# One program for two attention layers, and expert rows gathered inside the attention that follows

## Chip, cores and metric

The kernel runs on one core of a Trainium2 chip. The metric is the device time of one execution in microseconds (us).

## What is computed

Activations x of 8 batches x 256 tokens x 256 features (float32) pass four layers; each adds an attention over a context and then a feed-forward block, both on the layer-normalised x:

```python
x = x + _L0_xattn_ref(_layernorm(x, axis=-1), ctx_1024, ctx_1024, ...)
x = x + _L0_ffn_ref(_layernorm(x, axis=-1), ...)      # 16 gated experts, 2 per token
x = x + _L1_xattn_ref(_layernorm(x, axis=-1), ctx_1024, ctx_1024, ...)
x = x + _L1_ffn_ref(_layernorm(x, axis=-1), ...)      # 8 experts, the last of 2 chosen
x = x + _L2_xattn_ref(_layernorm(x, axis=-1), ctx_1024, ...)
x = x + _L2_ffn_ref(_layernorm(x, axis=-1), ...)      # attention of x to itself, routed
x = x + _L3_xattn_ref(...); x = x + _L3_ffn_ref(...)
```

The "feed-forward" block of layer 2 is itself an attention of 16 heads of 16:

```python
q_norm = q / jnp.linalg.norm(q, axis=-1, keepdims=True)
q_scaled = (q_norm + query_embedding[None]) * jax.nn.softplus(temperature)[None]
attn = jax.nn.softmax(jnp.einsum('bhqd,bhkd->bhqk', q_scaled, k) / math.sqrt(hd), axis=-1)
h = jnp.einsum('bhqk,bhkd->bhqd', attn, v)      # then merged to rows of 256
gates = jax.nn.softmax(h @ Wr.T + br, axis=-1)  # 3 of 15 are kept
sw = jax.nn.softmax(h @ Ws.T + bs, axis=-1)
out = (h * masked_gates.sum(axis=-1, keepdims=True)) @ Wp.T + bp
```

## The kernel before

The program is a sequence of stages, each a block in which PE, DVE, ACT, POOL and SP have their own instruction streams and meet by semaphores; no engine starts a stage before all have left the last. The order is load, **a0** (attention, `attention16`), **f0** (`sorted_gated_experts`), **a1** (retention, `retention16`), **f1** (`sorted_experts`), **a2** (`attention16` with biases), **f2** (`attention16` with keys and values from x, and with the router), **a3** (`attention64`), **f3** (`truncated_experts`), store. x stays in SBUF (`g.x`, "g_x_all") through all of them, 16 tiles of 128 tokens by 256; so do the statistics of each tile (`g.stats`).

**attention16** (L290) is a software pipeline over the 8 batches. `head_steps` (L274) writes out steps s = -1 to 12, each of 8 slots. A slot holds the scores of two heads of batch s-3 (L655), the maxima of two heads of batch s-2 (L634, reduced by DVE at L806), and the extras that a table lists by slot, with the number of batches they lag: normalise ("norm", POOL, L206), transpose ("xT", L230), projections q, k, v (L580, L587), out and the product with wo ("y", added to x at L215 or L836). Each engine walks through the same list in this order and does its own part, so an operation that waits holds back all behind it on its engine. SP moves q and the negated maxima through HBM ("q_out", "q_in", "neg0_out" and so on) to reach other partitions. With 8 batches, the first five steps fill the pipeline and the last five drain it. In the routed form each batch has besides: squares of q, their sums, and the roots by one POOL `pow` (L498) on 128x32, and the gate (logits, three largest, exponentials, factor), mostly on DVE. The stage begins with `norm_factors` (L170), which makes mean and inverse deviation of all 16 tiles at once on DVE, with one root on ACT, and with two memsets on POOL, of KP and v (L473, L474). The routed one computes softplus of the temperature first (L512 to L706).

**retention16** (L1208) has the same form; its q and k are added up from parts by DVE (L1518), and POOL splits them (L1329) and applies causal masks (L1336).

**The experts** (f0 at L1840, f1 at L2290) sort the tokens by expert: POOL scatters the rows of x to slots in HBM, the experts run over tiles of 128 slots, and their rows go to `y_slots`. At the end POOL gathers for every token its rows back with indirect DMAs of 128x256: two for each tile in f0 (L1994, 32 in all), one in f1 (L2426, 16). The loops that issue them are the last work of the stage; DVE weighs and adds the rows to x as halves or tiles land, and takes the statistics for the next norm.

## Time and profile before

| what | value |
|---|---|
| median of 3 runs (range) | 2100.21 us (2098.96 to 2108.5) |
| profiled execution: device time | 2091.46 us |
| profiled execution: span | 2089.7 us |
| PE busy (share of the span) | 1607.8 us (77%) |
| PE weight loads busy | 1235.2 us (59%) |
| DVE busy | 996.2 us (48%) |
| ACT busy | 674.8 us (32%) |
| POOL busy | 512.9 us (25%) |
| mean granted TensorE clock | 0.858 |

The span is the time between the first and last instruction in the trace; it lies 1.8 us under the execution's own time. Busy shares are means over all stages. By the first instruction of each stage the stages begin, in us from the span's start, at 16.0 (a0), 233.0 (f0), 475.9 (a1), 698.3 (f1), 969.3 (a2), 1205.3 (f2), 1507.9 (a3), 2032.4 (f3).

### The profile page before, as it was taken

How to read it: one execution, taken by the hardware profiler on the slowest of the kernel's cores; microseconds unless marked ns; L12 is line 12 of the kernel's file. 1: busy time of each engine (PE TensorE's matmuls, PEld its weight loads, DVE VectorE, ACT ScalarE, POOL GpSimd, SP SyncE). 2: the span in 40 equal slices, each digit the busy share in tenths (PEclk: the TensorE clock that was granted, in tenths of full speed). 3: DMA queues.
4: the chain of work that ended last, by engine and by line, in shares of the span. 5: the costliest groups of instructions: out<-in, count | busy, mean ns of one | idle time of the engine just before them, and what ended most of it. 6: DMA issues, size and time to landing. Idle time of an engine off the chain costs nothing. (4 is left out here: it accounts for less than half of the span.)

```text
span 2089.7 us, 33375 instructions
## 1 busy us (share of the span) xinstructions
PE 1607.8 (77%) x12250; PEld 1235.2 (59%) x12250; DVE 996.2 (48%) x2190; ACT 674.8 (32%) x1408; POOL 512.9 (25%) x583
## 2 busy tenths in 40 slices
PE   4898775905888519981699746888699999999976
PEld 2565654804566418871466434655478888888766
DVE  2675262524454422113366446776426554455542
ACT  1464342302555101111366413434332222222111
POOL 2110043052444020005331064431042223222110
PEclk8798797957999659995799967988799999999986
DMA  4230553435644258852756034442110000000001
GB/s 135 68 83 18 185 213 105 135 91 153 141 112 92 75 204 295 301 197 86 166 130 133 3 85 108 103 92 53 44 55 7 6 7 1 6 6 2 1 7 41
DMA packets 89430, 195.54 MB, mean 94 GB/s; under 512 B 13536, under 2 KB 62176, under 8 KB 80704
## 3 DMA queue, kind: packets, MB, share of 16 engines
q1 hardware_dynamic: 76352, 173.07, 28.9%
q0 software_dynamic: 4608, 12.59, 1.8%
q10 hardware_dynamic: 8320, 7.87, 1.1%
q8 instruction: 96, 1.57, 0.3%
q14 instruction: 54, 0.44, 0.1%
HBM read 136.47 MB, written 57.02 MB: 93 GB/s over the span
## 5 line engine op out<-in xcount | busy, mean ns | idle before, releaser
L806 DVE TENSOR_REDUCE a_sb_mx<-a_mx 128x2 f32<-128x512 f32 x256 | 164.8, 686 | 97.7 <-PE a_mx L634 97.4
L1161 DVE RECIPROCAL a_sb_rden<-a_ot 128x256 f32<-128x256 f32 x64 | 112.1, 1752 | 146.6 <-PE a_ot L1047 146.5
L558 ACT ACTIVATE a_sb_probs<-a_ex 128x512 f32<-128x512 f32 x256 | 139.2, 598 | 103.9 <-PE a_ex L655 103.3
L230 PE MATMUL a_gp<-g_ident,a_sb_xn 128*128 128x128 f32 x128 | 25.1, 329 | 163.0 <-POOL a_sb_xn L206 80.0
L230 PEld LDWEIGHTS a_gp<-g_ident,a_sb_xn 128*128 128x128 f32 x128 | 16.9, 165 | 167.5 <-DMA a_sb_bo<-a_bo 70.9
L806 DVE TENSOR_REDUCE f_sb_mx<-f_mx 128x2 f32<-128x512 f32 x128 | 82.2, 684 | 36.7 <-PE f_mx L634 36.3
L558 ACT ACTIVATE f_sb_probs<-f_ex 128x512 f32<-128x512 f32 x128 | 69.5, 597 | 71.5 <-PE f_ex L655 71.4
L990 ACT ACTIVATE a_sb_probs<-a_sc 128x512 f32<-128x512 f32 x64 | 38.2, 597 | 167.9 <-PE a_sc L1035 111.7
L959 POOL TENSOR_SCALAR_AFFINE_SELECT a_sb_probs<-a_sb_probs 128x256 f32<-128x256 f32 x128 | 49.2, 409 | 164.9 <-ACT a_sb_probs L991 164.8
L655 PE MATMUL a_ex<-a_sb_QP,a_sb_KP 49*128 49x256 f32 x512 | 68.1, 343 | 24.8 <-ACT a_sb_probs L558 21.3
L952 POOL TENSOR_TENSOR a_sb_q_lo<-a_sb_whole,a_sb_q_hi 128x512 fp32r<-128x512 f32 x32 | 40.7, 1271 | 180.0 <-ACT a_sb_q_hi L981 180.0
L2488 PE MATMUL f_hb<-f_sb_xsT,f_sb_wb 128*128 128x128 f32 x640 | 76.0, 281 | 10.9 <-ACT f_sb_xsT L2441 10.9
L2488 PEld LDWEIGHTS f_hb<-f_sb_xsT,f_sb_wb 128*128 128x128 f32 x640 | 74.3, 196 | 13.1 <-issue 6.6
L980 ACT ACTIVATE a_sb_whole<-a_gp 128x512 f32<-128x512 f32 x64 | 38.3, 598 | 134.5 <-PE a_gp L999 134.5
L655 PEld LDWEIGHTS a_ex<-a_sb_QP,a_sb_KP 49*128 49x128 f32 x512 | 42.2, 197 | 63.9 <-issue 40.2
L634 PE MATMUL a_mx<-a_sb_KP,a_sb_QP 48*128 48x256 f32 x512 | 62.7, 322 | 17.4 <-DVE a_sb_mx L806 16.3
L668 PE MATMUL a_ot<-a_sb_probs,a_sb_v 128*32 128x256 f32 x1024 | 74.1, 410 | 0.0
L2602 DVE TENSOR_SCALAR f_sb_hT<-f_hb,f_sb_wb 128x128 f32<-128x128 f32 x80 | 22.5, 344 | 105.3 <-PE f_hb L2488 105.3
L1336 POOL TENSOR_SCALAR_AFFINE_SELECT a_sb_sim<-a_sb_sim 128x256 f32<-128x256 f32 x128 | 49.9, 418 | 89.0 <-ACT a_sb_sim L1390 89.0
L2497 PE MATMUL f_yb<-f_sb_wb,f_sb_hT 128*128 128x256 f32 x320 | 70.7, 379 | 0.0
L1146 DVE TENSOR_REDUCE a_sb_mx<-a_sc 128x2 f32<-128x256 f32 (+1 forms) x128 | 62.1, 544 | 11.6 <-PE a_sc L1020 11.6
L2497 PEld LDWEIGHTS f_yb<-f_sb_wb,f_sb_hT 128*128 128x128 f32 x320 | 60.0, 190 | 7.7
(427 smaller groups left out, 3929.5 us busy)
## 6 DMA issues: line engine op xcount, KB each, us to landing
f_sb_wb<-f_w SPq DMA_DIRECT2D x20, 2052.0 KB, 11.3
a_sb_kvT<-ctxT SPq DMA_DIRECT2D x32, 256.0 KB, 3.5
a_q_moved<-a_sb_qs SPq DMA_DIRECT2D x16, 512.0 KB, 3.5
a_sb_QP<-a_q_moved SPq DMA_DIRECT2D x32, 256.0 KB, 4.7
f_x_slots<-f_sb_zero SPq DMA_DIRECT2D x1, 6144.0 KB, 20.1
f_sb_xs<-f_x_slots SPq DMA_DIRECT2D x20, 256.0 KB, 2.8
f_y_slots<-f_sb_ys ACTq DMA_DIRECT2D x20, 256.0 KB, 2.6
a_sb_QP<-a_q_moved SPq DMA_DIRECT2D x32, 128.0 KB, 5.0
```

The costliest lines, as they stand in the source:

```text
L230: op = pe.transpose(out[:, k, t * P:(t + 1) * P], xn[:, t, k * P:(k + 1) * P], g.ident[:])
L558: act.activation(probs[:, group % 3, 2 * (u % 2) + par], EX[par][:], ACT.Exp, scale=scale)\
L634: op = pe.matmul(MX[par][:, t, :], QP[at:at + R, b % 3, u, t * P:(t + 1) * P], KP[at:at + R, b % KB, u % KM, :], start=True, stop=True)
L655: op = pe.matmul(EX[par][:, t, :], KP[at:at + R + 1, b % KB, u % KM, t * P:(t + 1) * P], QP[at:at + R + 1, b % 3, u, :], start=True, stop= ...
L668: op = pe.matmul(OT[c // 2][32 * j:32 * j + 32, c % 2, :], v4[:, b % 4, t, (4 * c + j) % VH, :], probs[:, (4 * b + c) % 3, j, t, :], start ...
L806: dve.tensor_reduce(mx[:, :, column(2 * u + par)], MX[par][:], AX.X, ALU.max, negate=True)\
L959: op = pool.affine_select(later, later, [[0, 2], [1, P]], ALU.is_ge, 0.0, base=0, channel_multiplier=-1)
L1146: op = dve.tensor_reduce(mx[:, t, 2 * i:2 * i + 2], SC[pair][:, :, t, 0:(t + 1) * P], AX.X, ALU.max, negate=True)
L1161: dve.reciprocal(rden[:, n], OT[n][:, 1, :])
L1336: op = pool.affine_select(later, later, [[0, 2], [1, P]], ALU.is_ge, 0.0, base=0, channel_multiplier=-1)
L2488: op = pe.matmul(HB[j % 2][c // (FC // 2)][:, c % (FC // 2), :], w1(j, k, c), xsT[:, j, k, :], start=(k == 0), stop=(k == KD - 1))
L2497: op = pe.matmul(YB[j % 2][:, 0], hT[:, j, c, :], w2(j, c), start=(c == 0), stop=(c == FC - 1))
```

## The change

1. a2 and f2 become one call of `attention16` over 16 batches: batch 8+i is batch i of the routed layer, whose x is what batch i of a2 has left. The steps are 22 where they were 14 and 14. Both layers' weights lie in SBUF.
2. The gathers of f0 and f1 leave the experts' stages. `Arrival` issues them batch by batch on POOL within the first steps of a1 and of the merged stage, by the table `ARRIVALS` (step: batches gathered, batches added). DVE adds them and takes the statistics. Norm factors are then computed for one or two batches at a time by `batch_norm_factors`, with a Newton iteration instead of ACT's root: on DVE in a1, on POOL in the merged stage, there also for each routed batch.
3. The maxima of a pair of heads are one PSUM tensor and one DVE reduction of 128x1024 where two of 128x512 stood.
4. In routed batches the roots of q's sums are a Newton iteration on POOL (14 operations of 128x32) instead of one `pow`; squares and the copies of the negated maxima go from DVE to ACT; the query embedding is added as a bias of ACT's split of q; the gate's exponentials are six small ACT operations that also sum. "norm", "v" and "scale" change slots.
5. KP is filled by DVE; of v POOL fills columns 16 to 31 only.

Order of the instructions: POOL, from the tail of f0 into a1 (`sb_xn`, `sb_xnT` receive the first and second expert's rows). Before:

```order
L1994 DMA f_sb_xn<-f_y_slots,f_sb_pos 128x256
L1994 DMA f_sb_xnT<-f_y_slots,f_sb_pos 128x256
L1856 UNCONDITIONAL_BRANCH
L1321 UNCONDITIONAL_BRANCH
L1323 MEMSET a_sb_v 128x3072
L1329 TENSOR_TENSOR a_sb_q_parts<-a_sb_q_whole,a_sb_q_parts 128x512
L1329 TENSOR_TENSOR a_sb_k_parts<-a_sb_k_whole,a_sb_k_parts 128x512
L1344 TENSOR_TENSOR g_x_all<-g_x_all,a_sb_bo 128x512
L1329 TENSOR_TENSOR a_sb_q_parts<-a_sb_q_whole,a_sb_q_parts 128x512
```

With the change:

```order
L2146 UNCONDITIONAL_BRANCH
L1473 UNCONDITIONAL_BRANCH
L249 DMA a_sb_landing<-f_y_slots,g_pos 128x256 x16
L1482 TENSOR_TENSOR a_sb_q_parts<-a_sb_q_whole,a_sb_q_parts 128x512
L1482 TENSOR_TENSOR a_sb_k_parts<-a_sb_k_whole,a_sb_k_parts 128x512
L1497 TENSOR_TENSOR g_x_all<-g_x_all,a_sb_bo 128x512
L249 DMA a_sb_landing<-f_y_slots,g_pos 128x256 x8
L1482 TENSOR_TENSOR a_sb_q_parts<-a_sb_q_whole,a_sb_q_parts 128x512
L1482 TENSOR_TENSOR a_sb_k_parts<-a_sb_k_whole,a_sb_k_parts 128x512
L1497 TENSOR_TENSOR g_x_all<-g_x_all,a_sb_bo 128x512
L249 DMA a_sb_landing<-f_y_slots,g_pos 128x256 x8
```

The tail has no gather left; sixteen stand ahead of POOL's first split of q in a1, eight ahead of the second.

PE, where a2 gives over to f2 (`a_ex` scores, `a_mx` maxima, `a_gp` all small products). Before:

```order
L655 MATMUL a_ex<-a_sb_QP,a_sb_KP 128x256 x4
L587 MATMUL a_gp<-a_sb_wo,a_sb_oT 128x256 x4
L668 MATMUL a_ot<-a_sb_probs,a_sb_v 32x256 x8
L678 MATMUL a_gp<-g_ident,a_sb_oraw 128x128 x8
L230 MATMUL a_gp<-g_ident,a_sb_otm 128x128 x4
L587 MATMUL a_gp<-a_sb_wo,a_sb_oT 128x256 x4
L308 UNCONDITIONAL_BRANCH
L575 UNCONDITIONAL_BRANCH
L230 MATMUL f_gp<-g_ident,f_sb_xn 128x128 x4
L587 MATMUL f_gp<-f_sb_wq,f_sb_xnT 128x256 x4
```

With the change, the end of step 8, in which the first routed batch (8) enters, and the start of step 9:

```order
L305 MATMUL a_gp<-g_ident,a_sb_qtm 128x128 x4
L742 MATMUL a_gp<-a_sb_wo,a_sb_oT 128x256 x4
L806 MATMUL a_ex<-a_sb_QP,a_sb_KP 128x256 x4
L785 MATMUL a_mx<-a_sb_KP,a_sb_QP 128x256 x4
L305 MATMUL a_gp<-g_ident,a_sb_xn 128x128 x4
L794 MATMUL a_gp<-g_ident,a_sb_mx 8x128 x2
L819 MATMUL a_ot<-a_sb_probs,a_sb_v 32x256 x8
L806 MATMUL a_ex<-a_sb_QP,a_sb_KP 128x256 x4
L785 MATMUL a_mx<-a_sb_KP,a_sb_QP 128x256 x4
L742 MATMUL a_gp<-a_sb_wq,a_sb_xnT 128x256 x4
```

Batch 8's q is transposed beside batch 4's product with wo, and batch 9's transposes and q stand among the scores of batch 6 and the maxima of batch 7. Before, a2 had run empty before f2's first transpose.

POOL, one full step of routed batches. Before:

```order
L483 TENSOR_TENSOR f_sb_qs<-f_sb_qf,f_sb_qs 128x512
L498 TENSOR_TENSOR f_sb_qn<-f_sb_qn,f_sb_half 128x32
L483 TENSOR_TENSOR f_sb_ks<-f_sb_kf,f_sb_ks 128x512
L504 TENSOR_TENSOR g_x_all<-g_x_all,f_sb_bo 128x512
L206 TENSOR_SCALAR f_sb_xn<-g_x_all,g_ln_mean,g_ln_rstd 128x256 x2
```

With the change, from the norm on (L1338 to L1344 follow twice more, then L632, the bias L639 and the split of q):

```order
L209 TENSOR_SCALAR a_sb_xn<-g_x_all,g_ln_mean,g_ln_rstd 128x256 x2
L597 TENSOR_TENSOR a_sb_ks<-a_sb_kf,a_sb_ks 128x512
L1320 TENSOR_SCALAR a_sb_qn<-a_sb_qn 128x32
L1338 TENSOR_TENSOR a_sb_qn<-a_sb_qn 128x32
L1340 TENSOR_TENSOR a_sb_qn<-a_sb_qn 128x32
L1342 TENSOR_SCALAR a_sb_qn<-a_sb_qn 128x32
L1344 TENSOR_TENSOR a_sb_qn<-a_sb_qn 128x32
```

The `pow` (L498) gives way to 14 operations, and 21 more (L220 to L1344, on 128x2) stand ahead of each norm.

The diff, cut to its core:

```diff
+def batch_norm_factors(eng, g, first, last, ln):
+    at = slice(first * TT, (last + 1) * TT)
+    ln = ln[:, :, 0:at.stop - at.start]
+    st = lambda i: g.stats[:, at, i]
+    eng.tensor_tensor(ln[:, 0, :], st(1), st(4), ALU.add)
+    eng.tensor_tensor(ln[:, 1, :], st(1), st(4), ALU.subtract)
+    eng.tensor_tensor(ln[:, 2, :], st(2), st(5), ALU.add)
+    eng.drain()
+    eng.tensor_scalar(g.mean[:, at], ln[:, 0, :], 0.5, None, ALU.mult)
+    eng.tensor_tensor(ln[:, 1, :], ln[:, 1, :], ln[:, 1, :], ALU.mult)
+    eng.tensor_scalar(ln[:, 2, :], ln[:, 2, :], 1.0 / D, EPS, ALU.mult, ALU.add)
+    eng.drain()
+    eng.tensor_scalar(ln[:, 1, :], ln[:, 1, :], 0.25, None, ALU.mult)
+    eng.drain()
+    eng.tensor_tensor(ln[:, 3, :], ln[:, 1, :], ln[:, 2, :], ALU.add)
+    eng.drain()
+    root_guess(eng, g.rstd[:, at], ln[:, 3, :])
+    for _ in range(3):
+        root(eng, g.rstd[:, at], ln[:, 3, :], g.rstd[:, at], ln[:, 4, :])
...
+class Arrival:
+    def __init__(self, sb, sem, landed, layer):
+        self.layer, self.n = layer, 2 - layer
+        self.rows = sb("landing", [P, 2, self.n, TT, D])
+        self.landed, self.taken, self.arrived = landed, sem("taken"), sem("arrived")
+    def gather(self, pool, g, b):
+        at_least(pool, self.taken, b - 1)
+        for t in range(TT):
+            for i in range(self.n):
+                pool.indirect_dma_start(self.rows[:, b % 2, i, t, :], None, g.y_slots[self.layer],
+                                        bass.IndirectOffsetOnAxis(g.pos[self.layer][:, i, b * TT + t:b * TT + t + 1], 0))\
+                    .then_inc(self.landed[b % 2], 16)
+    def add(self, dve, g, b):
+        dve.wait_ge(self.landed[b % 2], 16 * TT * self.n * (b // 2 + 1))
+        xb = g.x[:, b * TT:(b + 1) * TT, :]
+        if self.layer == 1:
+            dve.tensor_tensor(xb, xb, self.rows[:, b % 2, 0], ALU.add).then_inc(self.taken, 1)
+            dve.drain()
+        else:
+            for i in range(2):
+                for t in range(TT):
+                    op = dve.scalar_tensor_tensor(out=xb[:, t], in0=self.rows[:, b % 2, i, t, :],
+                                                  scalar=g.weight[:, i, b * TT + t:b * TT + t + 1], in1=xb[:, t],
+                                                  op0=ALU.mult, op1=ALU.add)
+                if i == 1:
+                    op.then_inc(self.taken, 1)
+                dve.drain()
+        next_stats(dve, g, b).then_inc(self.arrived, 1)
+        dve.drain()
+ARRIVALS = {-1: ([0, 1], [0]), 0: ([2, 3], [1]), 1: ([4, 5], [2, 3]), 2: ([6, 7], [4, 5]), 3: ([], [6, 7])}
+def arrivals(s):
+    gathers, adds = ARRIVALS.get(s, ([], []))
+    return [("gather", b) for b in gathers] + [("arrive", b) for b in adds] + [("factors", b) for b in adds[-1:]]
...
-ROUTED_EXTRAS = {0: [("neg1", 3), ("xT", 0), ("weigh3", 4), ("y", 5)], 1: [("q", 0), ("square", 0), ("out1", 4)],
-                 2: [("weigh0", 3), ("T0", 4), ("T1", 4)], 3: [("k", 0)], 4: [("neg0", 2), ("weigh1", 3), ("aT", 4)],
-                 5: [("scale", 0), ("gate", 4), ("v", 0), ("out0", 3), ("norm", -1)], 6: [("weigh2", 3), ("gexp", 4)],
-                 7: [("qT", 0), ("factor", 4)]}
+ROUTED_EXTRAS = {0: [("neg1", 3), ("xT", 0), ("weigh3", 4), ("y", 5)], 1: [("q", 0), ("out1", 4), ("norm", -1)],
+                 2: [("square", 0), ("weigh0", 3), ("T0", 4), ("T1", 4)], 3: [("k", 0), ("sums", 0)],
+                 4: [("neg0", 2), ("weigh1", 3), ("aT", 4), ("roots", 0)], 5: [("gate", 4), ("out0", 3)],
+                 6: [("weigh2", 3), ("gexp", 4), ("v", 0), ("scale", 0)], 7: [("qT", 0), ("factor", 4)]}
...
+                    if what == "gather":
+                        rows_in_flight.gather(pool, g, b)
+                        if b == 1:
+                            fill_ones()
+                    elif what == "factors":
+                        pool.wait_ge(rows_in_flight.arrived, b + 1)
+                        batch_norm_factors(pool, g, first_of(b), b, ln)
+                    elif what == "norm":
+                        if b >= B:
+                            pool.wait_ge(stats_ready, b - B + 1)
+                            batch_norm_factors(pool, g, b % B, b % B, ln)
                         if b >= 1:
                             full(pool, "xT", b - 1)
-                        normalise(pool, g, b, xn, xn_ready)
-                    elif what == ("qT" if router else "q"):
+                        normalise(pool, g, b % B, xn, xn_ready)
...
-                    elif what == "square":
-                        pool.wait_ge(q_sums, b + 1)
-                        pool.tensor_tensor(qn[:, 2], qn[:, 0], half[:], ALU.pow).then_inc(q_roots, 1)
+                    elif what == "roots":
+                        r = b - of(b).first
+                        pool.wait_ge(q_summed, r + 1)
+                        if r == 0:
+                            pool.wait_ge(centre, 1)
+                        else:
+                            pool.wait_ge(q_scaled, r)
+                        root_guess(pool, qn[:, 3], qn[:, 0])
+                        for _ in range(3):
+                            root(pool, qn[:, 3], qn[:, 0], qn[:, 3], qn[:, 1])
+                        by_token = lambda a: a.rearrange("p (t h) -> p t h", t=TT)
+                        pool.tensor_tensor(by_token(qn[:, 2]), by_token(qn[:, 3]),
+                                           spq[:, 0:H].rearrange("p (a h) -> p a h", a=1).broadcast_to([P, TT, H]),
+                                           ALU.mult).then_inc(q_rooted, 1)
...
+                    elif what == "square":
+                        act.wait_ge(q_biased, b - of(b).first + 1)
+                        act.activation(qsq[:], qtm[:], ACT.Square).then_inc(q_squared, 1)
                     elif what == "qT":
-                        split_rows("qT", b, qf, qs, q_split, q_out, None)
+                        if b == of(b).first:
+                            act.wait_ge(centre, 1)
+                        split_rows("qT", b, qf, qs, q_split, q_out, qe)
+                    elif what.startswith("neg") and routed(b):
+                        half_ = number(what)
+                        full(act, what, b)
+                        if b >= 1:
+                            act.wait_ge(neg_out[half_], 16 * b)
+                        act.activation(negT[:, half_, :], GP[bank][0:8, 0, :], ACT.Copy).then_inc(gp_read[bank], 1)
...
-                        act.wait_ge(gate_in, b + 1)
-                        act.activation(le[:, :, 0:H + 1], lg[:, :, 0:H + 1], ACT.Exp).then_inc(gate_exp, 1)
+                        act.wait_ge(gate_in, b - of(b).first + 1)
+                        for t in range(TT):
+                            act.activation(le[:, t, 0:H - 1], lg[:, t, 0:H - 1], ACT.Exp, bias=neg_top[:, t, 0:1],
+                                           accum_out=sums[:, t, 0:1])
+                            act.activation(le[:, t, H + 1:H + 4], top[:, t, 0:3], ACT.Exp, bias=neg_top[:, t, 0:1],
+                                           accum_out=sums[:, t, 1:2])
+                            op = act.activation(le[:, t, H - 1:H + 1], lg[:, t, H - 1:H + 1], ACT.Exp,
+                                                bias=neg_top[:, t, 1:2], accum_out=sums[:, t, 2:3])
+                        op.then_inc(gate_exp, 1)
...
+                        at_least(pe, mx_read, 8 * b + u)
                         for t in range(TT):
                             for par in range(2):
                                 at = 64 * par
-                                op = pe.matmul(MX[par][:, t, :], QP[at:at + R, b % 3, u, t * P:(t + 1) * P],
+                                op = pe.matmul(MX[:, par, t, :], QP[at:at + R, b % 3, u, t * P:(t + 1) * P],
                                                KP[at:at + R, b % KB, u % KM, :], start=True, stop=True)
-                                if t == TT - 1:
-                                    op.then_inc(mx_full[par], 1)
+                                if t == TT - 1 and par == 0:
+                                    op.then_inc(mx_full, 1)
+                        op.then_inc(mx_full, 1)
...
-                            dve.wait_ge(mx_full[par], 8 * b + u + 1)
-                            dve.tensor_reduce(mx[:, :, column(2 * u + par)], MX[par][:], AX.X, ALU.max, negate=True)\
-                               .then_inc(mx_read[par], 1)
-                    elif what.startswith("neg"):
+                        dve.wait_ge(mx_full, 2 * (8 * b + u + 1))
+                        pair = mx[:].rearrange("p t (i g h) -> p g t i h", i=2, g=2)[:, :, :, u // 4, u % 4]
+                        dve.tensor_reduce(pair, MX[:], AX.X, ALU.max, negate=True).then_inc(mx_read, 1)
...
-            centre_values()
             for step in steps:
                 for what, b in step:
                     bank = gp.slot((what, b)) if what in small else None
-                    if what in ("qr", "kr"):
+                    if what == "arrive":
+                        rows_in_flight.add(dve, g, b)
+                    elif what == "factors":
+                        batch_norm_factors(dve, g, first_of(b), b, ln)
...
-            for half_ in range(2):
-                for t in range(half_ * NT // 2, (half_ + 1) * NT // 2):
-                    for i in range(2):
-                        pool.indirect_dma_start(rows[i][:, t, :], None, y_slots,
-                                                bass.IndirectOffsetOnAxis(pos[:, i, t:t + 1], 0))\
-                            .then_inc(gathered[half_], 16)
...
-            pool.wait_ge(scattered, 16 * NT)
-            for t in range(NT):
-                pool.indirect_dma_start(rows[:, t, :], None, y_slots, bass.IndirectOffsetOnAxis(pos[:, t:t + 1], 0))\
-                    .then_inc(gathered[2 * t // NT], 16)
...
-                attention16(nc, g, s, w, bias=True)
+                layers = [(sub(io, n + "_"), n == "f2") for n in ("a2", "f2") if n in stages]
+                attention16(nc, g, s, layers, arriving="f1" in stages)
-            elif s == "f2":
-                attention16(nc, g, s, w, bias=True, kv_from_x=True, router=True)
```

## Rows read from the trace of the kernel before

**Rows 1.** Busy time by stretch: us, PE, PEld, DVE, ACT, POOL busy (x), PEclk, DMA share, GB/s.
```profile
424.00:475.85 51.85, 0.00 (x0) 0.00 (x0) 18.44 (x48) 0.00 (x0) 30.42 (x32) 0.50 0.29 81
969.26:1205.30 236.04, 184.44 (x1440) 123.86 (x1440) 121.93 (x220) 113.18 (x228) 58.23 (x43) 0.88 0.45 106
1205.30:1508.50 303.20, 222.00 (x1536) 148.87 (x1536) 189.19 (x468) 114.47 (x225) 103.26 (x52) 0.79 0.32 76
1073.00:1136.80 63.80, 61.26 (x542) 41.51 (x544) 42.42 (x79) 41.04 (x84) 16.17 (x13) 1.00 0.57 131
1340.10:1400.90 60.80, 52.62 (x386) 34.81 (x384) 44.23 (x112) 26.77 (x54) 23.32 (x12) 0.84 0.41 94
```

**Rows 2.** Timeline, tail of f0: start, duration, engine, [idle before it <- what ended it].
```profile
423.54 0.98 POOL L1994 DMA_INDIRECT f_sb_xn<-f_y_slots,f_sb_pos  x1 [87.32 <-issue]
...
462.92 0.94 POOL L1994 DMA_INDIRECT f_sb_xnT<-f_y_slots,f_sb_pos  x1 [0.30 <-issue]
...
475.86 2.66 POOL L1323 MEMSET a_sb_v<- 128x3072 f32 x1 [11.99 <-POOLq L140]
```

**Rows 3.** Timeline, tail of f1 and the first work of a2.
```profile
940.80 0.97 POOL L2426 DMA_INDIRECT f_sb_rows<-f_y_slots,f_sb_pos  x1 [177.41 <-issue]
...
949.62 0.95 POOL L2426 DMA_INDIRECT f_sb_rows<-f_y_slots,f_sb_pos  x1 [0.30 <-issue]
...
952.34 2.29 DVE L2614 TENSOR_TENSOR g_x_all<-g_x_all,f_sb_rows 128x2048 f32<-128x2048 f32 x1 [15.07 <-DMA f_sb_rows<-f_y_slots,f_sb_pos]
953.37 2.08 POOL L2426 DMA_INDIRECT f_sb_rows<-f_y_slots,f_sb_pos  x1 [0.30 <-issue]
...
969.26 5.22 POOL L473 MEMSET a_sb_KP<- 128x6144 f32 x1 [7.55 <-POOLq L140]
969.76 4.75 DVE L177 TENSOR_SCALAR g_ln_mean<-g_ln_mean 128x16 f32<-128x16 f32 x1
```

**Rows 4.** Timeline, fill of a1: first transpose, then the q of batch 0 and batch 3.
```profile
488.28 1.12 PE L230 MATMUL a_gp<-g_ident,a_sb_xn 128*128 128x128 f32 x4 [70.51 <-DMA a_sb_bo<-a_bo]
...
497.58 0.69 DVE L1518 TENSOR_TENSOR a_sb_q_whole<-a_sb_part 128x512 f32<-128x512 f32 x1
...
543.89 0.69 DVE L1518 TENSOR_TENSOR a_sb_q_whole<-a_sb_part 128x512 f32<-128x512 f32 x1
```

**Rows 5.** Busy time of a1's first 68 us (columns of rows 1).
```profile
475.85:543.90 68.05, 48.10 (x300) 36.11 (x304) 26.94 (x49) 27.74 (x57) 24.00 (x34) 0.84 0.70 173
```

**Rows 6.** Timeline, fill of a2: transposes of batches 0 and 2.
```profile
981.24 1.12 PE L230 MATMUL a_gp<-g_ident,a_sb_xn 128*128 128x128 f32 x4 [44.43 <-POOL a_sb_xn L206]
...
1011.05 1.09 PE L230 MATMUL a_gp<-g_ident,a_sb_xn 128*128 128x128 f32 x4 [4.08 <-POOL a_sb_xn L206]
```

**Rows 7.** Timeline, what is added to x in a2: batches 0 and 7.
```profile
1073.02 0.69 DVE L215 TENSOR_TENSOR g_x_all<-g_x_all,a_gp 128x512 f32<-128x512 f32 x1 [0.74 <-PE a_gp L587]
...
1202.86 0.69 DVE L215 TENSOR_TENSOR g_x_all<-g_x_all,a_gp 128x512 f32<-128x512 f32 x1 [4.56 <-PE a_gp L587]
```

**Rows 8.** Timeline, the same in f2: batches 0 and 3, and the start of a3.
```profile
1340.09 0.87 DVE L836 SCALAR_TENSOR_TENSOR g_x_all<-f_gp,f_sb_sm,g_x_all 128x256 f32<-128x256 f32 x2 [2.17 <-PE f_gp L587]
...
1429.76 0.88 DVE L836 SCALAR_TENSOR_TENSOR g_x_all<-f_gp,f_sb_sm,g_x_all 128x256 f32<-128x256 f32 x2 [2.50 <-PE f_gp L587]
...
1507.93 0.18 DVE L173 TENSOR_TENSOR g_ln_mean<-g_ln_stats 128x16 f32<-128x16 f32 x1 [0.76 <-PEq L140]
```

**Rows 9.** Timeline of f2: end of its softplus chain; the roots of one batch.
```profile
1215.41 0.43 DVE L706 TENSOR_TENSOR f_sb_qe<-f_sb_qe,f_sb_spq 128x256 f32<-128x256 f32 x1
...
1345.63 5.45 POOL L498 TENSOR_TENSOR f_sb_qn<-f_sb_qn,f_sb_half 128x32 f32<-128x32 f32 x1 [10.28 <-DVE f_sb_qn L719]
```

**Rows 10.** Lines of POOL: busy us, mean ns of one | idle before.
```profile
L504 POOL TENSOR_TENSOR g_x_all<-g_x_all,f_sb_bo 128x512 f32<-128x512 f32 x8 | 10.2, 1279 | 0.0
L476 POOL MEMSET f_sb_half<- 128x32 f32 x1 | 0.1, 143 | 0.0
```

**Rows 11.** The page's costliest groups: the maxima of a0 and a2.
```profile
L806 DVE TENSOR_REDUCE a_sb_mx<-a_mx 128x2 f32<-128x512 f32 x256 | 164.8, 686 | 97.7 <-PE a_mx L634 97.4
```

412 lines of the change are left out of this document (216 added, 196 removed).

## Prediction

> **What bounds the kernel now.** The table of stages came first: no engine is busy throughout, and PE's 77% is a mean over stages of which some are bound by PE and some are not. So the stages that the change touches were read one by one, each by busy time in a window and then by the timeline at its ends.
>
> The tails of f0 and f1 are bound by one queue. In f0's last 51.85 us PE and ACT do nothing, POOL is busy for 30.42 us with 32 gathers, and DVE for 18.44 us with the adds and statistics [rows 1]. The first gather starts at 423.54 and the last, at a pitch of 1.25 us, at 462.92; a1 begins at 475.86 [rows 2]. In f1 16 gathers start at 940.80, and a2 begins at 969.26 [rows 3].
>
> a2 in its full steps is bound by PE: 61.26 us busy of 63.80 in three steps, with the clock at 1.00, so 21.27 us a step. f2 in its full steps is not: PE is busy 52.62 of 60.80 us at a clock of 0.84 and DVE 44.23, so a step takes 30.4 us while no engine fills it [rows 1]. The step holds a chain from engine to engine, of which one link is the `pow` on POOL, 5.45 us [rows 9]. Both stages also fill and drain: a2 takes 103.8 us from its start to its first y and f2 134.8 us [rows 1, 3, 7, 8].
>
> **The sum, part by part,** against the profiled execution (span 2089.7 us, device time 2091.46 us).
>
> *Gathers out of f0, into a1.* a1 starts when the experts' last rows are written, at about 424.3 in place of 475.86: 51.5 us less [rows 2]. Some comes back. Ahead of the first transpose, 12.4 us after a1's start now [rows 2, 4], stand four gathers at 1.25 us (5.0), the landing (1.8, from the eighth gather's end at 950.57 to the add at 952.34 [rows 3]), the adds and statistics of one batch (18.44 / 8 = 2.3 [rows 1]), 17 drained rounds of small operations at about 0.25 us (an estimate; the smallest single operation shown takes 0.18 [rows 8]), 4.3, and the norm: some 14.7, so +2.3. Behind it DVE does in steps 0 to 3 what it did in the tail, 2.3 us a batch, and four more sets of factors at 4.7 to 5.1: 7.0 + 3 x 9.7 = 36 us. a1's first 68 us have 41 us in which DVE is idle (26.94 busy of 68.05 [rows 5]), but PE is busy 48.10 of it and waits for DVE's q in order: the q of batch 0 to 3 are 46.3 us apart in sum [rows 4]. An add that waits for its landing holds the k and q sums queued behind it on DVE, and PE waits for those. I take 60% exposed, 22 us; the bounds are 10 (nearly all in the idle time) and 40 (all of it, and a wait). POOL's sixteen gathers end 20 us after the start, and its first split of q was due at 21.7 [rows 4], so POOL adds nothing there. **Net -27.5 us** (-39 to -9).
>
> *Gathers out of f1, into the merged stage.* The stage starts at 941.5 in place of 969.26. Its y of batch 0 came 103.8 us later; now the first transpose comes not 12.0 us after the start [rows 3, 6] but about 22.5: softplus stands ahead of the adds on DVE (its end is 10.6 us into f2 [rows 1, 9]; 12 with more loads), then add and statistics 1.6, 21 small POOL operations at 0.3 (below), 6.3, and the norm 2.5. The fill steps, 14.9 us from transpose to transpose [rows 6], get a POOL load of 4 gathers (5.0), factors (6.3), norm (2.5) and three operations of 1.28 [rows 10], 17.6 us: two steps give +5.4, and 1 for the third. So y of batch 0 comes at 941.5 + 103.8 + 17 = 1062.3, with 8 and 30 as bounds of the 17.
>
> A gather beside DVE's add of two SBUF operands took 2.08 us instead of 0.95 [rows 3]; eight of these would be 9 us more on POOL, within the upper bound. The Trainium skill ("SBUF — State Buffer", Who interferes with whom) has the two share one port pair that locks the loser out, but infers that this form of DVE operation leaves a gather's descriptors alone: those 9 us would then be nought. The trace speaks against that inference.
>
> *Fill and drain merged.* Three steps more with a2's work alone are 63.8 us [rows 1]: the end of step 7 is at 1126.1. Steps 8 to 15 carry in the same slots a routed batch coming in and an older one being scored. PE's work of a step in f2 is 26.3 us at clock 0.84, so 22.1 at full clock; DVE's is 22.1 (44.23 / 2) and loses squares, copies and gate operations; a2's step is 21.3 [rows 1]. The latency that made 30.4 us of it was the chain within one step; roots now have a slot of their own, v and scale come two slots later. I take 24 us, PE's 22.1 and gaps like a2's (2.5 in three steps) twice over: 192 us. The bounds are 21.3 and 30.4, 170 and 243. The drain from there is f2's: 78.2 us from its y of batch 3 to the start of a3 [rows 8], against 68.5 for the same stretch in a2 (1136.8 to 1205.3 [rows 1]); with the lighter gate I take 71. Together 1126.1 + 192 + 71 = 1389.1, in place of 1507.9. **-118.8 us** (-160 to -60).
>
> *Maxima.* Two reductions of 686 ns [rows 11] become one of about 1.3 us that starts when both halves are there. 192 pairs change, 64 of them in a0. DVE saves perhaps 0.07 us a pair and starts 0.1 later: 0, with -13 and +7 as bounds. *Memsets.* DVE's KP fill runs under the loads and beside softplus; POOL's goes. 0; without that cover it costs its 5.22 us once [rows 3]. *POOL's price.* No row shows an operation of two inputs on 128x32 or smaller. The ends are 0.14 us (a memset, no input) and 1.28 us (128x512, 16 times the columns) [rows 10]; I take 0.3, near the lower since the columns are few, with room for the drain. Roots and factors are 35 such, 10.5 us a step, on top of f2's 23.32 / 2 - 5.45 = 6.2 [rows 1, 9]: 16.7 us, under the 24.
>
> [...]
>
> Sum: -27.5 - 118.8 = -146.3, so 2091.5 - 146.3 = 1945.2 for the profiled execution. That one lay 8.7 under the median of the runs (2100.21), so **1954 us**.
>
> As a check: the merged stage would take 448 us, and a2 and f2 hold 184.4 + 222.0 = 406 us of busy PE, part of it at clocks of 0.88 and 0.79 [rows 1]. PE would be busy nine tenths of the time, which a2 alone reaches only in full steps; a higher clock shortens the 406, so it can be met, but not bettered by much.
>
> **The rivals.** *Cheaper than taken (0.13):* the routed step runs at a2's pace and a1 hides the adds: 8 x 2.5 + 10 = 30 less, 1924. For it speaks that PE's own work is 22.1; against it that f2's three full steps average 29.9 [rows 8]. *a1's fill gives it all back (0.08):* DVE waits for landings in order, and so do q and k; the 27.5 shrink to 0: 1982. For it, the 36 us on an engine on which PE's q depends; against it, DVE's 41 idle. *POOL becomes the pace of the merged stage (0.12):* it decides once 6.2 + 35p is over 24, from p = 0.51 us for a small drained operation. At p = 0.6 the step is 27.2 and the factors and roots of the fill and drain, 84 operations or so, cost 25 more: +51, 2005. For it speaks that the nearest two-input row is 1.28 and `pow` on the same tile takes 5.45; against it the memset's 0.14. *Slower (0.05):* the same operation at p = 0.86 or more: 8 x (35p - 17.8) + 84 x (p - 0.3) passes 146; at p = 1.0 it is 197, 2151. The place is POOL in steps 8 to 15, with PE waiting for transposes of xn. Only the distance of 1.28 from 0.3 allows it. *The forecast:* 0.62.
>
> **The numbers.** Range 1912 to 2012: the forecast with its bounds, the cheap case, a1's case and the milder half of POOL's. About 0.5% (10 us) is what a measurement of this kernel can tell from no change; only the slower case and the worst part of POOL's reach it. Faster 0.94, same 0.01, slower 0.05.
>
> **What would show it.** Small POOL operations under 0.35 us each; a routed full step of 23 to 25 us with PE's idle time below 3; the first transpose of a1 some 15 us and of the merged stage some 22 us after their starts; y of batch 0 about 121 us after the start. Wrong would be: PE in the merged stage waiting on POOL's xn at every step, a1 longer than 222.4 + 40 us, or a routed step near 30 with all engines partly idle, which would say that the chain and not the missing overlap set f2's pace.

## The result, and the profile after

The changed kernel takes 1969.81 us (median of 4 runs, 1968.33 to 1970.33) against 2102.89 us before (4 runs, 2098.96 to 2108.5). The ratio is 0.9364, its 95% interval 0.9339 to 0.9389: faster by 6.4%. Here and below, an execution over 1.5% longer than the fastest of its kernel is left out of the comparison; this concerns one of the run with two maxima and one of the kernel before. The forecast was 1954 us; the measured time lies 16 us above it, within the range.

The profiled execution took 1968.33 us, 123.1 less than the one of before. Its page, busy time of each engine:

```profile
span 1966.5 us, 33821 instructions
PE 1566.8 (80%) x12250; PEld 1211.7 (62%) x12250; DVE 956.5 (49%) x1948; ACT 688.7 (35%) x1527; POOL 533.5 (27%) x954
```

PE does the same 12250 products in 41 us less of busy time, at a mean clock of 0.88 in place of 0.858. The stages, from the first instruction of each, in us:

| stage | before | after | difference | forecast |
|---|---|---|---|---|
| a0 | 217.1 | 209.6 | -7.4 | 0 |
| f0 | 242.9 | 192.0 | -50.9 | -51.5 |
| a1 | 222.4 | 253.0 | +30.6 | +24 |
| f1 | 271.0 | 244.7 | -26.3 | -27.8 |
| a2 and f2, merged | 538.6 | 469.6 | -69.0 | -91 |
| a3, f3, store | 581.8 | 581.8 | 0.0 | 0 |

Busy time by stretch (columns as in [rows 1]) of a1's first 68 us, and of the merged stage: start to y of batch 0, three steps of a2's work alone, the eight steps with routed batches, the drain.

```profile
417.40:485.45 68.05, 28.72 (x116) 21.63 (x116) 45.62 (x147) 12.43 (x24) 39.18 (x40) 0.70 0.70 186
915.00:1048.50 133.50, 71.07 (x444) 50.35 (x446) 52.50 (x66) 40.86 (x86) 73.17 (x149) 0.73 0.56 138
1048.50:1111.46 62.96, 60.53 (x542) 41.23 (x544) 40.95 (x54) 40.98 (x84) 26.18 (x55) 1.00 0.58 132
1111.46:1304.50 193.04, 175.23 (x1532) 119.74 (x1534) 136.92 (x209) 123.20 (x294) 98.34 (x279) 0.99 0.48 109
1304.50:1384.68 80.18, 59.16 (x464) 37.35 (x462) 37.42 (x99) 38.18 (x109) 0.00 (x0) 0.83 0.13 28
```

The eight steps took 193.0 us where 192 were forecast: 24.1 each, PE busy 21.9 of them at a granted clock of 0.99. In f2 PE had been busy 26.3 of 30.4 us at 0.84 [rows 1], so the idle gaps are down from 4.1 to 2.2 us a step, and with the clock up the products themselves take 4.4 us less. The two ends are dearer than forecast: 133.5 us to the first y against 121, and 80.2 for the drain against 71. In a1 DVE is busy 45.6 of 68 us where it was 26.9 [rows 5], and PE only 28.7 where it was 48.1.

Timeline of the merged stage, POOL alone, from three of the fill steps (start, duration, then in brackets the idle time before and what ended it):

```profile
941.96 0.19 POOL L222 TENSOR_TENSOR a_sb_ln<-g_ln_stats 128x2 f32<-128x2 f32 x1
943.74 0.23 POOL L224 TENSOR_SCALAR g_ln_mean<-a_sb_ln 128x2 f32<-128x2 f32 x1 [1.59 <-issue]
...
960.42 0.94 POOL L249 DMA_INDIRECT a_sb_landing<-f_y_slots,g_pos  x1 [0.30 <-issue]
...
961.69 0.20 POOL L222 TENSOR_TENSOR a_sb_ln<-g_ln_stats 128x4 f32<-128x4 f32 x1
...
968.08 0.24 POOL L224 TENSOR_SCALAR g_ln_mean<-a_sb_ln 128x4 f32<-128x4 f32 x1 [6.18 <-issue]
...
984.94 0.96 POOL L249 DMA_INDIRECT a_sb_landing<-f_y_slots,g_pos  x1 [0.30 <-issue]
...
986.24 0.20 POOL L222 TENSOR_TENSOR a_sb_ln<-g_ln_stats 128x4 f32<-128x4 f32 x1
...
993.56 0.24 POOL L224 TENSOR_SCALAR g_ln_mean<-a_sb_ln 128x4 f32<-128x4 f32 x1 [7.13 <-issue]
```

Between L222 and L224 the code has one `drain`. Three times it follows on four gathers, and three times POOL stands still, 1.6, 6.2 and 7.1 us. How long the gathers of the second group were on their way, by the view of line L249 in that window:

```profile
DMA to landing us min/median/max: 7.3/8.7/9.5
```

The last of them started at 960.42 and took 7.3 us to land, so it was there at 967.7; the operation behind the drain started at 968.08. At the other two places the last gather started at 940.69 and 984.94 and took 2.7 and 8.3 us: there at 943.4 and 993.2, with the next operation at 943.74 and 993.56. Each time POOL goes on 0.3 us behind the last landing, so the drain seems to last until the gathers have landed. No engine is named as the releaser ("issue"), so this was a theory until an experiment had moved the gathers.

What PE sees of it are the transposes of batches 0, 1 and 2:

```profile
936.68 1.12 PE L305 MATMUL a_gp<-g_ident,a_sb_xn 128*128 128x128 f32 x4 [28.00 <-POOL a_sb_xn L209]
...
956.53 1.09 PE L305 MATMUL a_gp<-g_ident,a_sb_xn 128*128 128x128 f32 x4 [9.87 <-POOL a_sb_xn L209]
...
981.02 1.09 PE L305 MATMUL a_gp<-g_ident,a_sb_xn 128*128 128x128 f32 x4 [13.59 <-POOL a_sb_xn L209]
```

The first comes 21.6 us after the stage's start at 915.08, near the forecast 22.5. The next two follow at 19.9 and 24.5 us, not at 14.9 as in a2 before [rows 6], and each time PE has waited for POOL's norm.

In a1 the first add of batch 0, and the first transpose:

```profile
421.92 0.95 POOL L249 DMA_INDIRECT a_sb_landing<-f_y_slots,g_pos  x1 [0.30 <-issue]
...
428.53 1.84 DVE L262 SCALAR_TENSOR_TENSOR g_x_all<-a_sb_landing,g_weight,g_x_all 128x256 f32<-128x256 f32 x4 [9.39 <-DMA a_sb_landing<-f_y_slots,g_pos]
...
437.11 1.09 PE L305 MATMUL a_gp<-g_ident,a_sb_xn 128*128 128x128 f32 x4 [28.19 <-DVE a_sb_xn L209]
```

The fourth gather ended at 422.87 and its rows were there at 428.5, 5.7 us later and not 1.8. The DMA engines are busier here: 0.89 of the time from 418 to 430 us, with a1's weights among the loads, against 0.32 from 940.8 to 952.3 us in the old tail of f1. That this is the cause is likely, but no run shows it alone. The first transpose comes 19.7 us after a1's start, where it was 12.4 [rows 2, 4] and 14.7 had been forecast. The sums of q of batches 0 to 3 come 30.4, 49.0, 75.2 and 96.7 us after the start, before 21.7, 35.8, 50.4 and 68.0. The lag is 8.7 at the first, 24.8 at the third, 28.7 at the fourth, and 29 to 31 for the last four. It arises in the fill and stays.

Prices on POOL, from the view of line L1340 between 1232 and 1304 us (ns, shortest/median/longest, then the first and last start and the shape):

```profile
L1340 POOL TENSOR_TENSOR a_sb_qn<-a_sb_qn x9: 250/252/272, 1244.6 to 1296.2; 128x32 f32<-128x32 f32 x9
L1340 POOL TENSOR_TENSOR a_sb_ln<-a_sb_ln x6: 194/194/196, 1233.2 to 1260.4; 128x2 f32<-128x2 f32 x6
```

The maxima, from the page's costliest groups, 1223 ns a pair where two of 686 stood [rows 11]:

```profile
L951 DVE TENSOR_REDUCE a_sb_mx<-a_mx 128x4 f32<-128x1024 f32 x192 | 234.7, 1223 | 121.2 <-PE a_mx L785 118.7
```

### The profile page after: what moved, and what is told of

Same layout as the page of the kernel before. It is cut to its first block and busy times, and to the rows that moved or that the text cites. A ratio compares the mean times of both kernels' runs of the same rounds, so it can differ in the third digit from the quotient of the medians.

```text
span 1966.5 us, 33821 instructions
## 1 busy us (share of the span) xinstructions
PE 1566.8 (80%) x12250; PEld 1211.7 (62%) x12250; DVE 956.5 (49%) x1948; ACT 688.7 (35%) x1527; POOL 533.5 (27%) x954
## 5 line engine op out<-in xcount | busy, mean ns | idle before, releaser
L951 DVE TENSOR_REDUCE a_sb_mx<-a_mx 128x4 f32<-128x1024 f32 x192 | 234.7, 1223 | 121.2 <-PE a_mx L785 118.7
L706 ACT ACTIVATE a_sb_probs<-a_ex 128x512 f32<-128x512 f32 x384 | 208.8, 598 | 157.3 <-PE a_ex L806 156.7
L806 PE MATMUL a_ex<-a_sb_QP,a_sb_KP 49*128 49x256 f32 x768 | 98.9, 334 | 39.6 <-ACT a_sb_probs L706 29.0
L249 POOL DMA_INDIRECT a_sb_landing<-f_y_slots,g_pos x48 | 46.5, 970 | 288.6 <-POOLq L143 264.8
L305 PE MATMUL a_gp<-g_ident,a_sb_xn 128*128 128x128 f32 x160 | 29.6, 314 | 117.9 <-POOL a_sb_xn L209 76.6
L806 PEld LDWEIGHTS a_ex<-a_sb_QP,a_sb_KP 49*128 49x128 f32 x768 | 60.7, 190 | 94.6 <-issue 57.2
L819 PE MATMUL a_ot<-a_sb_probs,a_sb_v 128*32 128x256 f32 x1536 | 109.3, 404 | 2.1 <-ACT a_sb_probs L706 2.1
L785 PE MATMUL a_mx<-a_sb_KP,a_sb_QP 48*128 48x256 f32 x768 | 88.2, 306 | 13.1 <-DVE a_sb_mx L951 12.4
L785 PEld LDWEIGHTS a_mx<-a_sb_KP,a_sb_QP 48*128 48x128 f32 x768 | 62.3, 195 | 24.4 <-DVE a_sb_mx L951 17.1
L2739 DVE TENSOR_SCALAR f_sb_hT<-f_hb,f_sb_wb 128x128 f32<-128x128 f32 x80 | 22.5, 344 | 105.0 <-PE f_hb L2625 105.0
L597 POOL TENSOR_TENSOR a_sb_qs<-a_sb_qf,a_sb_qs 128x512 fp32r<-128x512 f32 x24 | 31.0, 1291 | 154.1 <-ACT a_sb_qs L661 97.1
```

The lines of the kernel that those rows point to most:

```text
L305: op = pe.transpose(out[:, k, t * P:(t + 1) * P], xn[:, t, k * P:(k + 1) * P], g.ident[:])
L706: act.activation(probs[:, group % 3, 2 * (u % 2) + par], EX[par][:], ACT.Exp, scale=scale)\
L785: op = pe.matmul(MX[:, par, t, :], QP[at:at + R, b % 3, u, t * P:(t + 1) * P], KP[at:at + R, b % KB, u % KM, :], start=True, stop=True)
L806: op = pe.matmul(EX[par][:, t, :], KP[at:at + R + 1, b % KB, u % KM, t * P:(t + 1) * P], QP[at:at + R + 1, b % 3, u, :], start=True, stop= ...
L819: op = pe.matmul(OT[c // 2][32 * j:32 * j + 32, c % 2, :], v4[:, b % 4, t, (4 * c + j) % VH, :], probs[:, (4 * b + c) % 3, j, t, :], start ...
L951: dve.tensor_reduce(pair, MX[:], AX.X, ALU.max, negate=True).then_inc(mx_read, 1)
```

## The experiments

All medians stand beside the change's 1969.81 us. Each run was timed against the kernel before on the same chip; that ratio and its interval are given, to be held against the change's 0.9364 (0.9339 to 0.9389). Lengths of stages are those of the one profiled execution.

**The merge undone.** a2 and f2 are two programs again, each in the new form:

```diff
-                layers = [(sub(io, n + "_"), n == "f2") for n in ("a2", "f2") if n in stages]
-                attention16(nc, g, s, layers, arriving="f1" in stages)
+                attention16(nc, g, s, [(w, False)], arriving="f1" in stages)
+            elif s == "f2":
+                attention16(nc, g, s, [(w, True)])
```

> The merge alone undone: a2 and f2 are again two programs of 8 batches, each in the new form, a2 still with its arrivals. Theory 1 (most of the merge's gain is a fill and a drain that overlap; the routed step of 24.1 us is a property of the routed form, not of the overlap): a2 takes about 133 + 63 + 68 = 264 us, f2 about 125 + 3 x 24 + 80 = 277, together 541 in place of 469.6: about +71, 2040 us. Theory 2 (the overlap itself gave the routed step its pace): f2's full steps are again 30 us and it takes 300, together 564: about +95, 2064 us.

Measured: 2038.03 us (ratio 0.9695, 0.9654 to 0.9737), theory 1's number. The two stages take 534.1 us in place of 469.6. In f2 alone, y of batches 0 to 2:

```profile
1296.47 0.87 DVE L980 SCALAR_TENSOR_TENSOR g_x_all<-f_gp,f_sb_factor,g_x_all 128x256 f32<-128x256 f32 x2 [4.03 <-PE f_gp L742]
1320.75 0.88 DVE L980 SCALAR_TENSOR_TENSOR g_x_all<-f_gp,f_sb_factor,g_x_all 128x256 f32<-128x256 f32 x2 [2.50 <-PE f_gp L742]
1345.18 0.87 DVE L980 SCALAR_TENSOR_TENSOR g_x_all<-f_gp,f_sb_factor,g_x_all 128x256 f32<-128x256 f32 x2 [2.50 <-PE f_gp L742]
```

24.3 and 24.4 us a step without any merge. So the merge as such is worth 64.5 us, one fill against one drain, and the step's pace belongs to the routed form: f2 by itself takes 277.2 us (1171.00 to 1448.21) where it took 302.6. In these two steps PE is busy 22.3 us each at a granted clock of 1.00, so the higher clock too comes with the routed form and not with the merge.

**f0's gathers back in a tail,** a block of their own between f0 and a1:

```diff
+                gather_tail(nc, g, "t0", 0)
-                retention16(nc, g, s, w, arriving="f0" in stages)
+                retention16(nc, g, s, w)
```

> The 32 gathers and adds of f0 stand in a tail of their own again, before a1, which starts with factors for all tiles. Theory 1 (a1 is 30.6 us longer because of the arrivals in its fill, and the tail was 51): a1 is back at 222 to 223 us, the sum about +20, 1990 us. Theory 2 (a1 is longer for another reason, its new memset or other edits): a1 stays near 253 and the whole is about +51, 2020 us.

Measured: 2001.52 us (0.9505, 0.9457 to 0.9553), +32. The tail takes 52.5 us. a1 takes 228.2, not the 222 to 223 of theory 1 and far from theory 2's 253. By the stages the arrivals save 52.5 + 228.2 - 253.0 = 27.7 us. Of the rest, a0 and a3 to the store are 3.6 and 3.3 us longer in this profile, and the edit touches neither. Where a1's 6 us over the kernel before come from is open: its q sums run level with before up to the fourth (69.1 us against 68.0), and the granted clock is 0.87 against 0.89.

**f1's gathers back in a tail,** by the same block for layer 1:

```diff
+                gather_tail(nc, g, "t1", 1)
-                attention16(nc, g, s, layers, arriving="f1" in stages)
+                attention16(nc, g, s, layers)
```

> The 16 gathers and adds of f1 stand in a tail of their own again, the rest is merged as before. Theory 1 (the fill of the merged stage gave all of it back: y of batch 0 came 133.5 us after the start in place of 103.8, the tail was 27): y of batch 0 comes about 107 us after the start, the whole is the same within 5 us, 1970 us. Theory 2, the prediction's (a gain of 27.8 - 17 = 11 us): 1981 us.

Measured: 1972.01 us (0.9389, 0.9345 to 0.9433), the same as the change. The tail takes 28.6 us, and y of batch 0 comes 100.3 us after the start of the merged stage where the change needs 133.5. This part of the change brought nothing: the fill took back what the tail gave.

This tail also has the slow gather of [rows 3] once more, beside the same add of 128x2048 with two operands in SBUF:

```profile
926.81 0.95 POOL L2763 DMA_INDIRECT t_rows<-f_y_slots,g_pos  x1 [0.30 <-issue]
927.05 2.29 DVE L2774 TENSOR_TENSOR g_x_all<-g_x_all,t_rows 128x2048 f32<-128x2048 f32 x1 [18.32 <-DMA t_rows<-f_y_slots,g_pos]
928.07 2.10 POOL L2763 DMA_INDIRECT t_rows<-f_y_slots,g_pos  x1 [0.30 <-issue]
```

It took 2.10 us, and 2.08 before. Both times it started while the add ran and ended 0.8 us behind the add's end, and both times the gather ahead of it, which met the add's beginning, kept its 0.95.

**Factors ahead of the gathers** on POOL, steps 0 to 3 of the merged stage:

```diff
-        steps = [arrivals(i - 1) + step for i, step in enumerate(steps)]
+        rank = {"factors": 0, "gather": 1, "arrive": 2}
+        steps = [(arrivals(-1) if i == 0 else sorted(arrivals(i - 1), key=lambda u: rank[u[0]])) + step
+                 for i, step in enumerate(steps)]
```

> One change of order on POOL in the merged stage: in steps 0 to 3 the factors of the batches added stand ahead of the next gathers, not behind them. Theory 1 (the first drain behind gathers lasts until they have landed: idle 1.6, 6.2 and 7.1 us before L224): these three waits go, y of batch 0 comes about 12 us sooner, about 1957 us. Theory 2 (that idle time is covered, or POOL waits there for something else): the same time within 3 us, 1969, with gaps that remain.

Measured: 1957.43 us (0.9306, 0.9268 to 0.9344), theory 1's number. The same two places of the timeline, where no gather is under way now:

```profile
960.61 0.19 POOL L222 TENSOR_TENSOR a_sb_ln<-g_ln_stats 128x4 f32<-128x4 f32 x1
961.31 0.24 POOL L224 TENSOR_SCALAR g_ln_mean<-a_sb_ln 128x4 f32<-128x4 f32 x1 [0.51 <-issue]
...
979.99 0.19 POOL L222 TENSOR_TENSOR a_sb_ln<-g_ln_stats 128x4 f32<-128x4 f32 x1
980.69 0.24 POOL L224 TENSOR_SCALAR g_ln_mean<-a_sb_ln 128x4 f32<-128x4 f32 x1 [0.51 <-issue]
```

0.51 us in place of 6.2 and 7.1, with the same instructions on the same tiles. y of batch 0 comes 122.1 us after the start, 11.4 sooner. The merged stage as a whole is only 7.4 us shorter in this profile (462.2), since the eight steps and the drain took 196.0 and 81.2 us; the profiled execution is the longest of the four (1966.07).

**Two maxima again,** in a0 and the merged stage:

```diff
-                        dve.wait_ge(mx_full, 2 * (8 * b + u + 1))
-                        dve.tensor_reduce(pair, MX[:], AX.X, ALU.max, negate=True).then_inc(mx_read, 1)
+                        for par in range(2):
+                            dve.wait_ge(mx_full[par], 8 * b + u + 1)
+                            dve.tensor_reduce(pair[:, par], MX[par][:], AX.X, ALU.max, negate=True)\
+                               .then_inc(mx_read[par], 1)
```

> Only the maxima undone: two PSUM tensors and two reductions of 128x512 for a pair of heads, in a0 and in the merged stage. Theory 1 (one reduction takes 1.22 us in place of 2 x 0.686, 0.15 saved a pair on an engine that is seldom last): a0 5 to 8 us longer, routed steps up to 1 us longer, together about +10, 1979 us. Theory 2 (the single reduction is what brought the routed step from 30 to 24 us): eight routed steps of 27 or more, +30 or more.

Measured: 1981.03 us, the middle of three from 1964.41 to 1986.02 (0.939, 0.9319 to 0.9462). The interval holds the change's 0.9364, so the times alone show no difference. In its profile a0 takes 217.0 us as before, steps of a2's work alone are 21.26 us, near the old length and not 20.97, and the eight steps with routed batches take 194.8 us against 193.0. So the single reduction gives 0.2 to 0.3 us a step of eight pairs and is not what brought 30 to 24; the 7 us in a0 agree with theory 1, but a0 also varied from 207 to 215 us between profiles of kernels that have it unchanged.

**One pow again** for the roots of the routed batches:

```diff
-                        root_guess(pool, qn[:, 3], qn[:, 0])
-                        for _ in range(3):
-                            root(pool, qn[:, 3], qn[:, 0], qn[:, 3], qn[:, 1])
+                        pool.tensor_tensor(qn[:, 3], qn[:, 0], half[:], ALU.pow)
+                        pool.drain()
```

> Only the roots of the routed batches changed: one power of -0.5 on POOL in place of the guess and three Newton steps (13 operations at a pitch of 0.34 us, 4.4 us). Theory 1 (the slot in the table matters, not the operation, since pow takes 5.45): the same time within 4 us, 1970 us, routed steps of 24 to 25. Theory 2 (the pow itself held f2's steps up): steps of 27 or more, +25 us and more. Theory 3 (small operations on POOL are what costs): faster by 5 us or more.

Measured: 1979.25 us (0.9424, 0.938 to 0.9468), +9.4, between theories 1 and 2; the interval just meets the change's. The merged stage is 9.2 us longer, and four routed steps in the middle are 26.3, 25.5, 25.3 and 23.3 us, in the change 24.3, 24.2, 23.2 and 23.5: about 1.2 us a step for an operation that takes 5.46 us against 13 that take 4.4.

**Squares and negated copies back on DVE** in routed batches:

```diff
-                        act.wait_ge(q_biased, b - of(b).first + 1)
-                        act.activation(qsq[:], qtm[:], ACT.Square).then_inc(q_squared, 1)
+                        dve.tensor_tensor(qsq[:], qtm[:], qtm[:], ALU.mult).then_inc(q_squared, 1)
+                        dve.drain()
```

and the copies likewise, by one branch of DVE for all batches.

> In the routed batches the square of q and the two copies of the negated maxima are DVE's again, not ACT's (0.69 + 2 x 0.40 us and a drain a batch). Theory 1 (f2's old step was long because DVE, 22.1 us busy and its drains, kept PE's maxima waiting; at 17.1 of 24.1 there is room for 1.6 more): up to +1 us a step, 1970 to 1978 us. Theory 2 (every us on DVE is on the path): +13 or more. Theory 3 (DVE does not matter): no change, with ACT's 1.5 us a step less.

Measured: 1975.91 us (0.9405, 0.9369 to 0.9442), +6 with a spread of 1969.85 to 1983.15. Theory 1's range, but theory 3 is not excluded: the two intervals overlap, and the merged stage is 472.8 us against 469.6.

**The old slots** with that work on DVE:

```diff
-ROUTED_EXTRAS = {0: [("neg1", 3), ("xT", 0), ("weigh3", 4), ("y", 5)], 1: [("q", 0), ("out1", 4), ("norm", -1)],
-                 2: [("square", 0), ("weigh0", 3), ("T0", 4), ("T1", 4)], 3: [("k", 0), ("sums", 0)],
-                 4: [("neg0", 2), ("weigh1", 3), ("aT", 4), ("roots", 0)], 5: [("gate", 4), ("out0", 3)],
-                 6: [("weigh2", 3), ("gexp", 4), ("v", 0), ("scale", 0)], 7: [("qT", 0), ("factor", 4)]}
+ROUTED_EXTRAS = {0: [("neg1", 3), ("xT", 0), ("weigh3", 4), ("y", 5)],
+                 1: [("q", 0), ("square", 0), ("sums", 0), ("roots", 0), ("out1", 4)],
+                 2: [("weigh0", 3), ("T0", 4), ("T1", 4)], 3: [("k", 0)], 4: [("neg0", 2), ("weigh1", 3), ("aT", 4)],
+                 5: [("scale", 0), ("gate", 4), ("v", 0), ("out0", 3), ("norm", -1)], 6: [("weigh2", 3), ("gexp", 4)],
+                 7: [("qT", 0), ("factor", 4)]}
```

> The routed batches' table of slots as it was (norm, scale and v in slot 5, square, sums and roots right behind q in slot 1), with squares and negated copies on DVE as in the run with DVE's work back. Theory 1 (the slots brought most of the 30.4 to 24.3, because DVE waits less in the middle of its maxima): routed steps of 27 to 30, 1995 to 2025 us. Theory 2 (the slots do not matter; the lighter gate and the roots do): steps near 25, within 5 us of that run's 1976.

Measured: 1997.72 us (0.9511, 0.9493 to 0.9528), 22 over the run with DVE's work back. y of three batches within the routed steps, and busy time between the first and the last:

```profile
1253.91 0.87 DVE L975 SCALAR_TENSOR_TENSOR g_x_all<-a_gp,a_sb_factor,g_x_all 128x256 f32<-128x256 f32 x2 [7.03 <-PE a_gp L734]
1282.28 0.88 DVE L975 SCALAR_TENSOR_TENSOR g_x_all<-a_gp,a_sb_factor,g_x_all 128x256 f32<-128x256 f32 x2 [5.62 <-PE a_gp L734]
1311.81 0.88 DVE L975 SCALAR_TENSOR_TENSOR g_x_all<-a_gp,a_sb_factor,g_x_all 128x256 f32<-128x256 f32 x2 [7.14 <-PE a_gp L734]
```

```profile
1253.91:1311.81 57.90, 48.68 (x386) 32.39 (x386) 36.30 (x71) 30.41 (x80) 27.74 (x80) 0.91 0.40 92
```

28.4 and 29.5 us a step, with DVE busy only 18.2 of them; the other steps are between 24 and 28, but for the one from the last y of a2 to the first routed one, 35.9 us (26.6 in the change). The eight steps take 222.9 us together, against 196.5 in the run with DVE's work back and 193.0 in the change. With the lighter gate but the old order much of f2's old pace is back, and the clock is down to 0.91 with PE's gaps. Moving the operations in the list is worth 22 us here, while what they cost on their engines (the two runs before) is worth 6 and 9 at most, each near what these times can tell. The run moves norm, squares, sums, roots, v and scale at once, so it doesn't say which move counts.

**One arrival in each step,** with the factors first:

```diff
-ARRIVALS = {-1: ([0, 1], [0]), 0: ([2, 3], [1]), 1: ([4, 5], [2, 3]), 2: ([6, 7], [4, 5]), 3: ([], [6, 7])}
+ARRIVALS = {-1: ([0, 1], [0]), 0: ([2], [1]), 1: ([3], [2]), 2: ([4], [3]), 3: ([5], [4]), 4: ([6], [5]), 5: ([7], [6]),
+            6: ([], [7])}
```

> Factors ahead of the gathers on POOL as in the run with that order (1957 us), and one batch arrives in each step (steps 0 to 6) in place of two in steps 1 to 3, in a1 and in the merged stage. Theory 1 (in a1 the arrivals of two batches, 9.7 us of DVE in one fill step, hold back q and k; one batch costs 6.6 and the rest falls where DVE has room): a1 about 8 us shorter, the merged stage 2 to 5, together about 1946 us. Theory 2 (DVE has no room in a1's full steps either, and three more sets of factors cost 4.3 each): a1 5 to 13 us longer, 1960 to 1970 us.

Measured: 1945.89 us (0.926, 0.9222 to 0.9299), theory 1's number. In a1 the table is all that differs from the change (POOL has no factors there): it takes 239.6 us, 13.4 less, and the merged stage 450.0 (469.6; 462.2 with the order alone). The q of batch 3 comes 82.9 us after a1's start in place of 96.7. Three more sets of factors are paid in full steps, where they cost less than what they take out of the fill.

**Batch 0 added ahead of the softplus,** on top of that:

```diff
+            if arriving:
+                rows_in_flight.add(dve, g, 0)
             if L[-1].router:
                 dve.wait_ge(first_in, first_all)
                 dve.wait_ge(softplus, 1)
```

> As the run with one arrival a step (1945.9 us), and in the merged stage batch 0 is added before DVE waits for the softplus, not behind it. Theory 1 (the rows of batch 0 have landed by about 3.5 us before the softplus ends, and the first transpose hangs on that add): y of batch 0 comes 3 us sooner, 1943 us, a difference that the stage's rows can show and the medians hardly. Theory 2 (the landing is later, or another wait is last): nothing.

Measured: 1937.03 us (0.9215, 0.9191 to 0.924), the fastest version. The first y comes 112.0 us after the stage's start in place of 115.4, the 3 us foreseen; the median fell by 9, of which a1 and the merged stage show 2.4, so the rest is most likely the spread of that other run (1938.19 to 1951.87). That version is faster than the change by 33 us.

**a1's factors on POOL,** on top of one arrival a step:

```diff
                     elif what == "factors":
-                        batch_norm_factors(dve, g, first_of(b), b, ln)
+                        pool.wait_ge(rows_in_flight.arrived, b + 1)
+                        batch_norm_factors(pool, g, first_of(b), b, ln)
+                        pool.sem_inc(factored, 1)
```

DVE's norm waits for `factored`, and the factors stand ahead of each step's gathers in a1 too.

> As the run with one arrival a step, and in a1 the norm factors of each batch are POOL's, ahead of its gathers, not DVE's. Theory 1 (a1's fill is bound by DVE, which gets 4.3 us a batch back): a1 5 to 15 us shorter than 239.6, 1931 to 1941 us. Theory 2 (the chain from the add to the norm counts, and 21 operations at a pitch of 0.34 take 7.1 us where DVE's took 4.5): a1 5 to 20 us longer, 1951 to 1966 us.

Measured: 2013.11 us (0.9606, 0.9572 to 0.9641). Theory 2, and three times as bad as it said: a1 takes 304.8 us in place of 239.6. Two of its waits from the start of a1 to 550 us:

```profile
DVE a_sb_xn L209 <- POOLq L1348: 36.5, 5, 8.2
PE a_ot L1638 <- POOL a_sb_sim L1499: 24.4, 3, 12.4
```

DVE's norm waits for POOL five times, 7.3 us on average, about what a set of 21 operations takes. What the expectation had not priced comes on top: POOL's masks of the scores (L1499) stand in order behind the factors, and PE waits up to 12.4 us for them. In the same window POOL itself waits 23.0 us, in six pieces, for DVE's statistics ahead of its sets, and all behind them in its queue waits too.

**The arriving batches' factors on DVE in the merged stage,** on top of the fastest version:

```diff
-                        batch_norm_factors(pool, g, first_of(b), b, ln)
+                        pool.wait_ge(factors, b + 1)
...
+                        batch_norm_factors(dve, g, b, b, ln)
+                        dve.drain()
+                        dve.sem_inc(factors, 1)
```

> As the run with batch 0 added first (1937 us), and in the merged stage the norm factors of the eight arriving batches are DVE's, right behind each add, as in a1; POOL keeps the routed batches' factors. Theory 1 (in the fill the chain from add to norm counts, as a1 with POOL's factors showed from the other side, and DVE does the set in 4.5 us against POOL's 7.1): y of batch 0 about 5 to 10 us sooner, 1929 us. Theory 2 (DVE's maxima and v of the fill then wait behind it as much as the chain gains): the same within 3 us. Theory 3 (DVE, in order, becomes what PE waits for): +5 us or more.

Measured: 1972.97 us (0.939, 0.936 to 0.9419), 36 slower than without this edit; theory 3. In the profile the merged stage has 474.1 us in place of 447.8. The first y comes 122.8 us after the start (112.0) and the next two steps are 29.0 and 29.6 us. Waits between 950 and 1010 us:

```profile
POOL a_sb_landing L249 <- DVEq L926: 19.2, 3, 8.8
PEld a_mx L787 <- DVE a_sb_mx L959: 17.0, 6, 4.6
```

POOL's wait for DVE's factors stands ahead of the next gathers and delays them, and PE waits for DVE's maxima. This edit has both in it, and the run does not part them.

## Why the prediction was right, and where a term was off

*The tails.* "51.5 us less" and "27.8": right, 50.9 and 26.3 [rows 2, 3].

*What a1 gives back,* forecast 24, measured 30.6. The exposed adds and factors were sized rightly: 22 forecast, and the lag grows by 20 to 22 us behind the first q. Off was the first term, "the landing (1.8 ...)": it was read from a tail in which little else moves, and in a1 it took 5.7 beside the weights' loads. That the spread of arrivals, not DVE's total, sets the price was not foreseen: one batch a step gave 13.4 us back.

*The merged fill,* forecast +17 on 103.8, measured +29.7. This is the step that failed most. The first transpose came as forecast (21.6 us, 22.5 forecast); what was off are the steps behind it, 19.9 and 24.5 us where 17.6 had been taken. "21 small POOL operations at 0.3 (below), 6.3" came to 21 at a pitch of 0.34, 7.1. But the fill step's POOL load of 17.6 us left out that a drain behind gathers waits for their landing, 14.9 us in three steps; with the order turned, 11.4 of the 12.7 too many are gone. The bound of 30 just held it. With 27.8 - 17 = 11 us this part was still called a gain; it was none, as the run with the tail shows.

*The eight routed steps,* 24 us: right, 24.1, and for the reason given in part. "Roots now have a slot of their own, v and scale come two slots later" names the order, and the run with the old slots bears out that the order counts, though not which move of it. By the two tables v and scale come one slot later, from 5 to 6, and norm, squares and sums have moved as well. That it stood under the heading of fill and drain merged was wrong: the pace is there without the merge. The merge itself is worth 64.5 us and the routed form 25.4 in f2 alone.

*The drain,* forecast 71, measured 80.2 against f2's 78.1: "with the lighter gate I take 71" failed. DVE was busy 42.5 us in f2's drain and 37.4 in this one, yet the time did not follow. ACT's wait for aT's transposes is as long as ever, from the waits of the drain, before and after:

```profile
ACT f_sb_oT L570 <- PE f_gp L230: 13.3, 4, 7.2
```

```profile
ACT a_sb_oT L718 <- PE a_gp L305: 12.9, 4, 7.5
```

In the twelve other profiles with the lighter gate the drain is between 76.5 and 84.4 us, so 71 was reached by none. That the chain from scores to y sets the drain and not the gate is argued from this; no run tried it.

*Maxima,* forecast 0: PE bounds a2's steps, which still became 0.3 us shorter; a0 became 7.4 shorter, of which the runs don't say how much is chance.

*The price on POOL.* 0.3 us was taken; measured 0.25 for 128x32 and 0.19 for 128x2, with a pitch of 0.34 where a drain stands between. A routed step's POOL load was 12.3 busy and about 17 with the drains, under the 24. The rival in which POOL sets the pace did not come true there. The mechanism is real all the same, and came in the run with a1's factors on POOL: in its first 134 us DVE waited 36.5 us for the sets of 21 themselves, and PE 24.4 us for what stood queued behind them.

The Trainium skill ("GPSIMD Engine Reference", Elementwise — side-by-side cycle accounting) has about 2.6 cycles an element for an operation of two inputs, at 1.2 GHz. By it an estimate is 1.11 us for 512 columns and 0.07 for 32. The traces have 1.28 [rows 10] and 0.25, so both times 0.17 to 0.18 us are on top, and the 0.19 of two columns is nearly all of this kind. A drain adds 0.15 us between two operations (0.34 of pitch against 0.19).

*A gather beside DVE's add.* The bound let eight gathers take 1.1 us longer each. None did: all 48 took between 942 and 1227 ns. But the three longest, 1.11, 1.11 and 1.23 us where the median is 0.95, ran beside DVE operations with two operands in SBUF (adds of 128x256 and a product of 128x512), and the run with f1's tail has the long one again, 2.10 us beside the add of 128x2048. In the run with one arrival a step others took 0.97 beside adds of 128x256, so what small adds cost is little or nothing. The Trainium skill's inference ("SBUF — State Buffer", Who interferes with whom), that such an add leaves a gather's descriptors alone, is not borne out by the two long ones. The prediction's doubt of it was right; its bound of 1.1 us each was not reached, with adds that have become small.

Altogether: 7 in f0 and a1, 1.5 in f1, 12.7 in the fill and 9.2 in the drain less favourable than forecast, 7.4 in a0 more, which makes 23 of 146.3 - 123.1 us.

## What to carry to other kernels

Two pipelines that follow each other are worth merging by the fill and the drain that then overlap, here 64.5 us; read that from the busy time of the two stretches. Work taken out of an idle tail is only won if the next stage's fill has room for it on each in-order engine: spread it one batch a step, and look at what is queued behind each wait. Keep a drain off POOL's queue while it has gathers under way, or put the drained work ahead of them.

## Hardware behaviour that had not been expected

A `drain` on POOL behind indirect gathers lasted until the gathers' rows had landed (idle 1.6, 6.2 and 7.1 us, each time to 0.3 us behind the last landing), and 0.16 to 0.52 us where none was under way.

From its start to its landing a gather took 2.7 to 10.1 us within these pipelines, with a median of 6.5. In the old tail of f1 it had taken 2.7 by the same measure (949.62 to 952.34 [rows 3]; the 1.8 of the prediction counts from the gather's end). The short ones go with idle DMA engines: 2.7 to 2.9 us from 936 to 944 at a DMA share of 0.23, 7.3 to 9.5 from 956 to 968 at 0.94, 8.1 to 10.1 from 981 to 994 at 0.81.

An indirect gather beside a DVE add of 128x2048 with both operands in SBUF took 2.08 and 2.10 us in two kernels where its neighbours took 0.95.
